# One-hot matrices for a graph kernel's message sums: built by VectorE comparisons in place of ScalarE distances

## The reference

```python
scores = jnp.einsum('ehd,ehd->eh', q[dst], k[src]) * scale
m = jax.ops.segment_max(scores, dst, num_segments=n)
ex = jnp.exp(scores - m[dst])
z = jax.ops.segment_sum(ex, dst, num_segments=n)
attn = ex / z[dst]
agg = jax.ops.segment_sum(attn[:, :, None] * v[src], dst, num_segments=n)
```

## Time and profile before

| | |
|---|---|
| median of 3 runs | 6206.65 us (6206.27 to 6207.05) |
| span of the profiled execution | 6223.3 us |
| first edge stage, about | 455 to 2180 us |
| second edge stage, about | 3295 to 5040 us |
| busy over the span | PE 71%, DVE 63%, POOL 56%, ACT 40% |

### The profile page before, as it was taken

How to read it: one execution, slowest core, us unless ns; L and a number is a source line. 1 busy time by engine, 2 the same in 40 slices (tenths; PEclk the granted TensorE clock), 3 DMA queues, 4 the chain that set the end, 5 groups by cost and what they waited for, 6 DMA issues and landing times. The chain is left out here.

```text
span 6223.3 us, 97835 instructions
## 1 busy us (share of the span) xinstructions
PE 4414.7 (71%) x18128; PEld 3261.7 (52%) x18129; DVE 3938.5 (63%) x11481; ACT 2497.0 (40%) x7105; POOL 3454.4 (56%) x3249
## 2 busy tenths in 40 slices
PE   0686777777777767677586777777777767676768
PEld 0344455555555556666544555555555556666635
DVE  3686777777777744444386777777777754444446
ACT  0114555555555522222213555555555533222211
POOL 1215555555555458888724555555545548888844
PEclk9897888888888878888797888888888878888879
DMA  8335555555555556666535555555555555666655
GB/s 159 109 122 181 177 170 172 172 172 171 177 172 176 155 112 110 120 115 115 108 109 169 174 172 174 180 170 170 174 173 174 174 113 110 121 111 120 112 148 170
DMA packets 657743, 930.82 MB, mean 150 GB/s; under 512 B 143789, under 2 KB 481341, under 8 KB 657693
## 3 DMA queue, kind: packets, MB, share of 16 engines
q0 software_dynamic: 263808, 538.03, 36.4%
q1 hardware_dynamic: 363357, 364.47, 19.0%
q10 hardware_dynamic: 30528, 27.80, 1.4%
HBM read 804.64 MB, written 125.36 MB: 149 GB/s over the span
## 5 line engine op out<-in xcount | busy, mean ns | idle before, releaser
L734 POOL DMA_INDIRECT kv<-kv_scratch,src_u x1792 | 1745.4, 974 | 1660.4 <-DVE msg L885 1238.1
L1021 PE MATMUL sum_p<-msg,hot_s 128*128 128x273 f32 x3584 | 1250.9, 479 | 292.0 <-DVE msg L885 216.4
L1217 POOL DMA_INDIRECT sum_scratch<-ysum,dest x800 | 1242.7, 1553 | 233.2 <-issue 175.1
L1010 PE MATMUL qe<-queries,hot_q 128*128 x3584 | 1151.4, 452 | 220.8 <-issue 178.6
L1021 PEld LDWEIGHTS sum_p<-msg,hot_s 128*128 128x128 f32 x3584 | 725.7, 222 | 608.7 <-issue 356.0
L1010 PEld LDWEIGHTS qe<-queries,hot_q 128*128 128x128 f32 x3584 | 791.1, 226 | 455.2 <-issue 277.4
L870 DVE TENSOR_TENSOR prod<-qe,kv 128x512 f32<-128x512 f32 x896 | 614.1, 685 | 318.4 <-issue 256.5
L751 ACT ACTIVATE S<-qe 128x16 f32<-128x16 f32 x896 | 172.2, 192 | 1420.2 <-remote 673.9
L895 DVE TENSOR_TENSOR sums<-sums,sum_p 128x273 f32 x896 | 385.9, 431 | 423.1 <-remote 397.8
L877 DVE TENSOR_REDUCE S<-prod 128x16 f32<-128x512 f32 x896 | 610.6, 681 | 4.6
L885 DVE TENSOR_TENSOR msg<-kv,W 128x512 f32<-128x512 f32 x896 | 611.5, 683 | 3.1 <-PE sum_p L1021 3.1
(11 more groups left out here) (214 smaller groups left out, 6100.8 us busy)
## 6 DMA issues: line engine op xcount, KB each, us to landing
drow<-drel_scratch SPq DMA_DIRECT2D x224, 512.0 KB
ea<-in_edge_attr SPq DMA_DIRECT2D x104, 512.0 KB
srow<-in_src_rows SPq DMA_DIRECT2D x104, 512.0 KB
kv<-kv_scratch,src_u POOLq DMA_INDIRECT x1792
kv_scratch<-res SPq DMA_DIRECT2D x100, 256.0 KB, 2.0
hin<-h_scratch SPq DMA_DIRECT2D x158, 128.0 KB
h_scratch<-res SPq DMA_DIRECT2D x150, 128.0 KB, 1.7
hin<-h_scratch ACTq DMA_DIRECT2D x108, 128.0 KB
```

What stands on the lines that cost most here:

```text
L734: g.indirect_dma_start(out=kv[:, slot, :], out_offset=None, in_=KVd, in_offset=bass.IndirectOffsetOnAxis(ap=src_u[:, par, u:u + 1], axis=0 ...
L1010: ins = pe.matmul(qe[g % 2][:, u, 0:QW], hot_q[:, q % 2, (2 * g + u) % 4, :], queries[:, bass.ds(tile * QW, QW)], start=True, stop=True)
L1021: ins = pe.matmul(sum_p[g % 2][:, 0:XW], hot_s[:, (j // 2) % 2, (2 * j + u) % 4, :], msg[:, g % 2, u, :], start=(u == 0), stop=(u == 1))
L1217: g.indirect_dma_start(out=sum_d[r], out_offset=bass.IndirectOffsetOnAxis(ap=dest[:, k, j:j + 1], axis=0), in_=ysum[:, k, j, :], in_offset ...
```

## The change

The two ACT passes for `hot_s` go, and with them the semaphore `far_s_s` and the rule that orders the two users of `far`. DVE makes the four matrices of a quad instead, each by one comparison: (column + (-destination)) == 0, 128 x 128 float32 out of SBUF into SBUF. The comparisons stand in the steps 0, 2, 4 and 6 behind `products`, ahead of `messages`, `scores` and `add`. SP's load of `ndrel_u` now waits for the matrices themselves. In the profile of before the lines are numbered as in the function listing above; in the changed kernel `hot_for_sums` is L861, `messages` L871, `scores` L853, `add` L881.

```diff
-                far_q_s, hot_q_s, far_s_s, hot_s_s = s.many(4)
+                far_q_s, hot_q_s, hot_s_s = s.many(3)
...
-                            wait(sp, far_s_s, n * 4 - 4)
+                            wait(sp, hot_s_s, n * 4 - 4)
                             sp.dma_start(ndrel_u[:, par, :], a).then_inc(ndrel_in[par], 16)
...
-                        def hot_for_q(n, q, others):
+                        def hot_for_q(n, q):
...
-                            wait(a, hot_s_s, others)
...
-                        def hot_for_sums(m, par, loads, q, others):
-
-                            c = m * 4 + q
-                            a.wait_ge(ndrel_in[par], loads * 16)
-                            wait(a, hot_s_s, c)
-                            wait(a, hot_q_s, others)
-                            for u in range(4):
-                                ins = a.activation(far[:, u * P:(u + 1) * P], iota_f[:, :], ACT.Abs,
-                                                   bias=ndrel_u[:, par, q * 4 + u:q * 4 + u + 1])
-                            ins.then_inc(far_s_s, 1)
-                            a.wait_ge(far_s_s, c + 1)
-                            wait(a, sum_s, c * 2 - 2)
-                            a.activation(hot_s[:, q % 2, :, :].rearrange("p u e -> p (u e)"), far[:, :], ACT.Relu,
-                                         bias=ones[:, 0:1], scale=-1.0).then_inc(hot_s_s, 1)
...
-                                    hot_for_q(n, g // 2 + 2, n * 4 - 4 + g // 2)
+                                    hot_for_q(n, g // 2 + 2)
                                 elif g in (5, 7) and has_scores(n + 1):
-                                    hot_for_q(n + 1, g // 2 - 2, n * 4 - 4 + g // 2)
-                                elif g % 2 == 0 and message(n, 3 if g == 0 else 4):
-                                    others = n * 4 + 2 + g // 2
-                                    if isinstance(n, int):
-                                        others = min(others, NB * 4)
-                                    if g == 0:
-                                        hot_for_sums(n - 2, par, t, 3, others)
-                                    else:
-                                        hot_for_sums(n - 1, 1 - par, t + par, g // 2 - 1, others)
+                                    hot_for_q(n + 1, g // 2 - 2)
                                 if g == 3 and has_chain(n):
                                     a.wait_ge(delta_s, n)
...
+                        def hot_for_sums(m, par, loads, q):
+
+                            v.wait_ge(ndrel_in[par], loads * 16)
+                            wait(v, sum_s, m * 8 + q * 2 - 2)
+                            for u in range(4):
+                                ins = v.tensor_scalar(out=hot_s[:, q % 2, u, :], in0=iota_f[:, :],
+                                                      scalar1=ndrel_u[:, par, q * 4 + u:q * 4 + u + 1], scalar2=0.0,
+                                                      op0=ALU.add, op1=ALU.is_equal)
+                            ins.then_inc(hot_s_s, 1)
+
                         def messages(n, par, g, back, j):
...
                                         chain_edges(n)
                                 if has_scores(n):
                                     products(n, par, t, g)
+                                if g % 2 == 0 and message(n, 3 if g == 0 else 4):
+                                    if g == 0:
+                                        hot_for_sums(n - 2, par, t, 3)
+                                    else:
+                                        hot_for_sums(n - 1, 1 - par, t + par, g // 2 - 1)
                                 mj = message(n, g)
                                 if mj and g != 4:
                                     messages(n, par, g, *mj)

```

More of the change, by code:

```diff
@@ L832, in period @@
                                                  ACT.Copy).then_inc(w_s, 1)
-                        hot_for_q(0, 0, 0)
-                        hot_for_q(0, 1, 0)
+                        hot_for_q(0, 0)
+                        hot_for_q(0, 1)
                         own_scores(0, 0, 0)
```

## The result

The changed kernel took 6239.85 us (median of 4 runs, 6238.45 to 6244.54) against 6206.85 us before: 1.0046 of it, 95% interval 1.0032 to 1.0061. It is slower, as forecast, by 33 us and not by 170. That holds for the chip of this comparison. On another chip, in the experiment `after_again`, the changed kernel took 6023 us and the kernel before 5579 us, a ratio of 1.0795 (1.0777 to 1.0813). Most of what follows is about these two numbers.

What follows compares the result with a forecast made beforehand. No engine was full; PE, DVE and the wait between blocks bound successive stretches. DVE's 0.86 plus PE's 0.8 less ACT's 0.1 gave 1.55 us a block, 170 us over 110 blocks: median 6376 us, range 6110 to 6690.

Steps and rivals of the forecast that it cites:

- The price of a comparison: Each of DVE's 16 added comparisons a block was put at 0.219 us, 0.88 us for a quad of four.
- no gather shuts one out: Rival: comparisons and POOL's gathers block each other, a quad in step 6 waiting a whole gather; 6690 us, chance 0.08.
- Steps 4 and 6: DVE-bound stretch: 1.32 us in step 4 (0.44 wait plus 0.88 quad) and 0.88 in step 6, 2.20 a block.
- Step 2: DVE's quad of 0.88 us hidden in 1.3 us of idle time waiting for PE; uncovered, 97 us in all.
- Step 0: Block's start: comparisons, messages and scores, 2.08 us, now come after the late sum of step 7; scan 0.86 us later.
- the hold: Wait between two blocks in which PE's results become visible several us late and everything then resumes at once.
- PE behind it: PE's sum of step 0 and spread for step 2 now follow the late message: 0 or 1.6 us, taken as 0.8.
- The sum: 0.86 + 0.8 less 0.1 for ACT: 1.55 us a block, 170 us over 110 blocks.
- the boundary: Between two blocks: POOL stops after eight gathers, the wait ends earlier, giving back 1.3 of 2.20 us.
- the 0.1 credited to ACT: Gain from removing ACT's two passes, 0.1 us a block; bound 0.3 us a block, 35 us in all.
- no hold at the boundary: Rival: POOL never runs back to back long enough; 5990 us, half of blocks 6100; chance 0.24 with an unfalling PE clock.
- the gathers' run sets the hold: Reading that the late-semaphore wait at the block's start lasts while POOL issues gathers back to back, ending 2.8 us after the last.

Runs made afterwards that it cites:

- after_again: The changed kernel itself, unaltered, beside the kernel before on a chip without the hold: 6023.5 us, 1.0795 of the kernel before.
- half_gathers: The kernel before with the second of each pair of POOL's gathers left out from the third block on, on a chip with the hold: 5609.4 us, 0.914.
- pause_before: The kernel before with POOL pausing before a block's fifth pair of gathers until DVE has taken up the previous block's scores: 6050.0 us against 6130.5, 0.9863.
- pad_stage_one: The changed kernel with 92 one-column memsets on VectorE ahead of the first layer's edge loop, moving the loops' code: 5982.6 us, kernel before 5587.5.
- before_act_light: The kernel before with ScalarE's two passes for the sums' one-hot matrices cut to one column from the second block on: 5573.2 us, 0.9977.

## Why the prediction was wrong

- *The price of a comparison:* right. 0.219 us each, 393 us for 1792, and no gather shuts one out: the longest of all takes 0.508 us.
- *Steps 4 and 6:* the sum was right, 2.23 us measured over the steps 4 to 6 for 2.20 forecast. Its parts were not: 0.87 for 1.32 in step 4, 1.07 for 0.88 in step 6, 0.29 in step 5, for which nothing was forecast. Where PE's clock is full all through the step, step 4 grows by 0.76 us only (36 blocks of 42) and step 5 not at all (2.55 us, 30 of 42); the rest is PE at half clock. That the sum fits is in part luck.
- *Step 2:* the idle time did hide the quad on the chip of the result (5.00 to 4.71 us). But it was hidden behind a slow PE: step 2 took 5.09 us in the 37 of 42 blocks that the kernel before ran at half clock throughout, and 4.68 in the 11 blocks of the changed kernel with the full clock. On a chip without a hold, where this step ran at full clock, it took 3.92 us before and 4.69 with the quad, so there the quad cost 0.77. So the cover of 1.3 us reads as DVE's wait for PE at half clock; no run changes the clock alone.
- *Step 0:* **this step failed.** The prediction said "in the hold this sum is not visible" and put 2.08 us of work behind the hold in every block. In 37 of 50 blocks the sum had come before the hold began. The mechanism that it described, quad late, POOL stopped after eight gathers, hold ended 2.8 us after (2.7 measured), is there in 11 blocks. The steps 7 and 0 together shrank by 2.15 us where the forecast's terms give 1.34 (2.20 less 0.86).
- *PE behind it* (+0.8): **this term failed too**, and by more. The steps 1 to 3 shrank by 0.43 us together. The forecast took the middle between a full and a half clock on top of what was there; in the traces the clock in these steps rose, from 0.53, 0.54 and 0.66 to 0.71, 0.83 and 0.89. That fits the shorter steps, but it is not shown to be the cause.
- *The sum:* steps 4 to 6 +2.23, the rest of the block -2.56, so -0.33 us a block in the first stage where +1.55 was forecast. Of the miss of 1.9 us, 1.2 is the term for PE and 0.8 the boundary; the 0.1 credited to ACT goes the other way. The rival "no hold at the boundary" named what does it, POOL no longer running back to back, and priced half of the blocks at 6100 us. In the first stage 10 of 50 blocks lost the hold, 11 kept one of 5.2 us and 29 one of 7.4; the mean fell by 1.98 us, which with the faster PE paid for the comparisons and left hardly a gain. That the gathers' run sets the hold was the reading of few blocks on which the forecast turned, and it was right (`half_gathers`, `pause_before`).
- *Not in the sum at all:* VectorE's loop went from 260 to 301 records a pass. In the second stage its code came to lie where each branch back waits for a fetch, and the block takes 30.77 us, 0.26 more than before.

In the traces the first edge stage (first gather to last addition) fell from 1735.6 to 1725.5 us and the second rose from 1731.7 to 1756.3: +14.5 us, as good as the whole difference of the two spans (15.4). The medians lie 33 us apart because the profiled execution of before was 16.6 us over its median.

So the forecast's +170 is the answer for neither chip. Where there is no hold the comparisons cost 2.8 us a block, 310 to 320 us, and the stalls another 86 us (`pad_stage_one`) to some 130 (`after_again`, by the ratios, across chips); where there is one, its shortening pays for them.

## What to carry to other kernels

Before costing work added to an engine, ask what the block's longest wait depends on: here it moved by as much as the work itself. When an engine's loop body grows, look at the page's row of the instruction queue and at the time across the branch in every copy of the loop, and compare variants step by step, lengths and granted clock, before comparing their times: the half-clock stretch can move into the step that you made shorter. Time a kernel on more than one chip before calling a difference of half a per cent its own.

## What I had not expected of the hardware

- The same kernel takes 5579 to 5588 us on three chips and 6131 to 6228 in the four other comparisons. Outside the edge stages the stretches agree (the one between them: 1101.4 to 1108.3 us). Most of it is the hold: a block takes 30.52 us on the chip of the result and 24.57 in `before_act_light`, and of these 5.95 us step 0, in which the hold lies, has 4.44. Step 2 has 1.08, at a granted clock of 0.54 against 1.00, and step 7 has 0.54.
- In the held blocks PE's semaphores reach other engines up to 5 us late while GpSimd issues gathers of 0.95 us with 0.30 us between them, and come all at once 2.3 to 2.9 us after the last one's start (the middle, kernel by kernel). Messages from DVE to PE and POOL pass meanwhile. Half the gathers, or a pause, and it ends. Why they are late, and why only on some chips, stays open.
- A branch back on VectorE takes 0.4 us up to the next register load, or 3.7 to 8.0 on the mean of a stage, depending on where the loop's code lies.
- Time saved on VectorE came back as PE's half clock. Step 5 takes 2.55 us in the blocks with the full clock and 3.5 to 4.2 on the mean in the others, in each of six variants on the chips without a hold (for one, 2.55 and 4.17 in `before_act_light`, 34 and 8 blocks).
